# Layer 1's key chain: four split float32r products a head, or weights multiplied first in plain float32

## The chip, the cores and the metric

The kernel runs on one core of a Trainium2 chip. The metric is the device time of one execution in microseconds (us): before the change the median of 3 runs is 1177.97 us (1175.52 to 1180.46). The profiled execution took 1178.59 us and its recorded span is 1176.8 us, so 1.79 us lie around the span.

## The reference, cut to what matters

Four layers follow each other, each with an attention over a short context and a feed-forward stage; the stages run one after the other. The change lies in the attention of layer 1. Its mathematics, for 16 heads h, on the context `kv_rope` (4 batches of 64 rows, 64 wide, with the rotary tables applied):

```python
q_hk   = (hidden_q @ Wq.T).reshape(b, s, H, K)            # Wq: (16*128, 256)
q_big  = einsum('bshk,hkq->bshq', q_hk, w_kc_q)           # w_kc_q[h]: 128 x 192
q_r    = einsum('bshq,hqr->bhsr', q_big, W_qr)            # W_qr[h]: 192 x 64
k_r    = einsum('bld,hdr->bhlr', kv_rope, W_kr)           # W_kr[h]: 64 x 64
scores = einsum('bhsr,bhlr->bhsl', q_r, k_r)
attn   = softmax(scores)
ctx_c  = einsum('bhsl,bld->bhsd', attn, kv_rope)
out    = einsum('bhsd,hkd->bshk', ctx_c, w_kc_kv).reshape(b, s, H*K) @ Wo.T
```

Layer 1 puts no rotation on the queries, so everything that does not depend on them can be folded to the side of the keys: G[h] = Wq[h].T · w_kc_q[h] · W_qr[h] · k_r[h].T, a 256 x 256 block a head (256 model columns; 4 batches of 64 context rows), and Y[h] = w_kc_kv[h].T · Wo[:, h].T. The scores are then the normed x times G.

## The kernel before, in words

`latent_chain` (line 1056) computes G and Y before layer 1's attention. It takes the 16 heads in 4 rounds of two pairs, four heads a round. Every operand exists as two float32r tiles, a high part and the remainder, and `mm3` (line 79) forms a product as high·high + high·low + low·high, three matmuls.

Per round TensorE runs 14 steps: two steps of keys `KR` (W_kr by the context, 128 rows to 64), two of `Y`, four of `UU` (W_qr by KR, 64 rows to 96 twice), two of `VV` (w_kc_q by UU, 96 rows) and four of G (Wq by VV, 128 rows). That is 32 products of 256 columns, 96 matmuls. They go to the four PSUM banks of `PB` in turn. After each step ScalarE copies the bank to the high part (line 1122 or 1124) and VectorE subtracts it from the bank for the low part (line 1144 or 1147). The next step in the chain waits for that low part (`free`, line 1157).

The weights of a round come in four sections on SyncE's queue (line 1100) into one buffer `W`, whose memory is the tile STAGE and is shown as ffn_STAGE. ScalarE copies each section to `WS_hi` (`high`, line 1111) and GpSimd subtracts for `WS_lo` (line 1107); TensorE waits for `w_lo`. The next round's section may be loaded when GpSimd has split the last one. ScalarE does this splitting between its evictions, at the steps named in `AFTER`. GpSimd, ScalarE, VectorE and TensorE run their rounds in hardware loops, TensorE with its first round written out.

The layer's norm (`norm`, line 203) is done ahead of the rounds: ScalarE takes the standard deviation (line 235), VectorE normalizes 8 tiles (line 223), TensorE transposes them in 16 matmuls into the banks `NB` (line 247), ScalarE and VectorE split them (lines 240 and 229). Nothing in the rounds needs the result; `attend` (line 1202), which follows behind a barrier of all engines, does: its first score matmul reads G and the transposed x.

Of the kernel before, what the change touches and what calls it, by code (L numbers as in the profile page):

```python
# [15 lines left out]
P = 128  # L16
F32 = mybir.dt.float32
# [3 lines left out]
ALU = mybir.AluOpType  # L21
# [8 lines left out]
H = 16  # L30
# [13 lines left out]
CQ_N = {0: 2 * CQ, 1: 2 * 2 * K}  # L44


def pair_columns(layer):
    o_kr = O_CQ + CQ_N[layer]
# [37 lines left out]
def program(nc, A, out, rows_dram):  # L86
    with ExitStack() as top:
# [165 lines left out]
        def latent_rope(Y, AT):  # L253


            o_qr, o_kr, o_ck, o_wo, width = pair_columns(0)
# [799 lines left out]
        def latent_chain(GS, Y, W):  # L1056


            o_qr, o_kr, o_ck, o_wo, width = pair_columns(1)
            with ExitStack() as ctx:  # L1060
                WS = split(ctx, "WS", [P, 2, width])
                KR = split(ctx, "KR", [P, 4, B * L])
                UU = split(ctx, "UU", [ROT, 4, 2, B * L])
                VV = KR
                PB = psum(ctx, "PB", [P, 4, 512])
                NB = psum(ctx, "NB", [P, 4, 512])
                nrm = norm(ctx, "a1", [NB[:, j, :] for j in range(4)])

                SECTIONS = (slice(o_kr, o_qr), slice(o_qr, width), slice(O_CQ, o_kr), slice(O_WQ, O_CQ))
                NS = len(SECTIONS)  # L1070
                w_in = [sem(ctx, f"w_in_{c}") for c in range(NS)]
                w_hi, w_lo = sem(ctx, "w_hi"), sem(ctx, "w_lo")
                in_ps, part_hi, part_lo = sem(ctx, "in_psum"), sem(ctx, "part_hi"), sem(ctx, "part_lo")
                STEPS = 2 + 2 + 4 + 2 + 4
                ROUNDS = NP // 2

                def place(s, g):

                    if s < 2:
                        return R, 512, [part[0:R, 2 * s:2 * s + 2, :].rearrange("p h n -> p (h n)") for part in KR]  # L1080
                    if s < 4:
                        return P, D, [part[:, bass.ds(g * (2 * D) + (s - 2) * D, D)] for part in Y]
                    if s < 8:
                        return ROT, 512, [part[:, s - 4, :, :].rearrange("p q n -> p (q n)") for part in UU]
                    if s < 10:
                        return P, 512, [part[:, 2 * (s - 8):2 * (s - 8) + 2, :].rearrange("p h n -> p (h n)") for part in VV]
                    return P, 512, None

# [1280 lines left out]
```

## Time and profile before

| | |
|---|---|
| median of 3 runs | 1177.97 us |
| lowest, highest | 1175.52, 1180.46 us |
| profiled execution, its own time | 1178.59 us |
| its span | 1176.8 us |
| granted TensorE clock, mean over the span | 0.918 |
| PE busy | 1000.2 us |
| stage of the chain, from the last matmul of the stage ahead to the first score matmul | 577.4 to 649.74 us |

Engines are PE (TensorE's matmuls), PEld (its weight loads), DVE (VectorE), ACT (ScalarE), POOL (GpSimd) and SP (SyncE, DMA queue). A granted clock of 0.5 is TensorE at 1.2 GHz and 1.0 at 2.4 GHz. The ends of matmuls are modelled and overlap, so the step from one start to the next tells what one costs. A plain float32 matmul leaves two records (two weight loads and two passes), a float32r one leaves one; float32r tiles are often shown as f32. A "window" row gives busy time of each engine and its count of instructions in a stretch.

### The profile page before, as it was taken

To read this page: it belongs to the slowest core of one execution; us is meant where nothing else is said; L and a number is where in the kernel's file an instruction comes from. 1 tells how busy PE (TensorE), PEld (TensorE's weight loads), DVE (VectorE), ACT (ScalarE), POOL (GpSimd) and SP (SyncE) were. 2 spreads that over 40 slices of the span, in tenths; PEclk is the share of its full clock that TensorE was granted. 3 is DMA by queue.
4 is the path that set the end of the run, shared out by engine and by line. 5 is a ranking of instruction groups with operands and counts; after the bars stand their busy time and mean duration, and the time that the engine had idled before them with its cause. 6 is when DMAs were issued, how large, how long until landed. Compare 5 with 4: busy or idle time off the path is not lost. (4 is left out here: it accounts for less than half of the span.)

```text
span 1176.8 us, 14937 instructions
## 1 busy us (share of the span) xinstructions
PE 1000.2 (85%) x5309; PEld 809.6 (69%) x5309; DVE 690.7 (59%) x1133; ACT 387.6 (33%) x589; POOL 394.5 (34%) x258
## 2 busy tenths in 40 slices
PE   2999999867879999999688895967826769999997
PEld 2778787667669988888688794755715656566664
DVE  5466666455475655555556797967677864222221
ACT  2234342232413333333277432433313332211221
POOL 2576766300212222222075120153226320512222
PEclk9899999979889999999789997869966997999999
DMA  4111110001101111110242101000010009622220
GB/s 125 58 38 39 50 64 0 1 1 53 45 27 45 45 45 45 45 45 18 80 162 80 72 1 32 1 1 1 1 41 1 1 24 402 263 63 39 40 36 10
DMA packets 22817, 62.85 MB, mean 53 GB/s; under 512 B 4465, under 2 KB 13954, under 8 KB 20418
## 3 DMA queue, kind: packets, MB, share of 16 engines
q1 hardware_dynamic: 18690, 58.00, 14.1%
q0 software_dynamic: 4080, 4.22, 2.1%
q8 instruction: 30, 0.49, 0.2%
q14 instruction: 17, 0.14, 0.0%
HBM read 56.94 MB, written 9.21 MB: 56 GB/s over the span
## 5 line engine op out<-in xcount | busy, mean ns | idle before, releaser
L791 ACT ACTIVATE ffn_HG<-ffn_G,ffn_UB 128x512 f32<-128x512 f32 x54 | 37.1, 690 | 160.5 <-PE ffn_U L83 160.1
L761 POOL TENSOR_TENSOR ffn_WDS_lo<-ffn_WD,ffn_WDS_hi 128x1024 fp32r<-128x1024 f32 x9 | 22.1, 2457 | 200.3 <-ACT ffn_WDS_hi L781 200.3
L908 DVE SCALAR_TENSOR_TENSOR ffn_HF<-ffn_U,ffn_BIAS,ffn_HG 128x512 f32<-128x512 f32 x54 | 40.4, 751 | 82.6 <-ACT ffn_HG L791 82.4
L81 PE MATMUL ffn_DN<-ffn_WDS_hi,ffn_HS_hi 128*128 128x256 f32 x288 | 83.7, 290 | 3.9 <-DVE ffn_HS_lo L916 3.3
L2158 PE MATMUL ffn_GU<-ffn_W,ffn_XTB 128*128 x184 | 85.0, 605 | 0.3 <-issue 0.3
L82 PE MATMUL ffn_DN<-ffn_WDS_lo,ffn_HS_hi 128*128 128x256 f32 x288 | 83.3, 289 | 0.0
L83 PE MATMUL ffn_DN<-ffn_WDS_hi,ffn_HS_lo 128*128 128x256 f32 x288 | 83.2, 289 | 0.0
L923 DVE SCALAR_TENSOR_TENSOR X<-ffn_DN,ffn_CG,X 128x256 f32<-128x256 f32 x144 | 67.3, 481 | 20.6 <-PE ffn_DN L83 12.5
L1978 POOL DMA_INDIRECT out_x<-ffn_YB,ffn_XB x23 | 35.9, 1560 | 113.8 <-DVE ffn_YB L2107 111.8
L458 DVE TENSOR_TENSOR attn_RP<-attn_QB,attn_COS 96x1024 f32<-96x1024 f32 x32 | 39.0, 1217 | 51.3 <-PE attn_QB L83 51.2
L2096 DVE COPY ffn_XTB<-ffn_XP 128x256 f32<-128x256 f32 x23 | 9.8, 425 | 88.1 <-PE ffn_XP L2167 88.1
L81 PEld LDWEIGHTS ffn_DN<-ffn_WDS_hi,ffn_HS_hi 128*128 128x128 f32 x288 | 57.1, 198 | 5.2 <-DVE ffn_HS_lo L916 3.5
L564 PE MATMUL attn_ST<-attn_RP,attn_U 96*128 96x256 f32 x256 | 60.3, 385 | 0.0
L2185 PE MATMUL ffn_DN<-ffn_W,ffn_HT 128*128 (+1 forms) x248 | 58.7, 380 | 0.8 <-ACT ffn_HT L2003 0.8
L2158 PEld LDWEIGHTS ffn_GU<-ffn_W,ffn_XTB 128*128 128x128 f32 x184 | 33.1, 189 | 36.2 <-issue 33.7
L82 PEld LDWEIGHTS ffn_DN<-ffn_WDS_lo,ffn_HS_hi 128*128 128x128 f32 x288 | 57.2, 199 | 0.6
L83 PEld LDWEIGHTS ffn_DN<-ffn_WDS_hi,ffn_HS_lo 128*128 128x128 f32 x288 | 57.1, 198 | 0.0
L81 PE MATMUL attn_QB<-XT_hi,attn_C_hi 128*96 128x512 f32 x128 | 55.9, 437 | 1.2 <-DVE attn_C_lo L449 1.2
L1107 POOL TENSOR_TENSOR chain_WS_lo<-ffn_STAGE,chain_WS_hi 128x1024 fp32r<-128x1024 f32 (+2 forms) x16 | 42.4, 2665 | 37.6 <-ACT chain_WS_hi L1113 37.4
L350 POOL TENSOR_TENSOR attn_RP<-attn_RP,attn_RS 96x512 f32<-96x512 f32 x32 | 41.0, 1282 | 34.8 <-DVE attn_RS L462 34.8
L564 PEld LDWEIGHTS attn_ST<-attn_RP,attn_U 96*128 96x128 f32 x256 | 48.1, 193 | 6.6
L83 PE MATMUL attn_QB<-XT_hi,attn_C_lo 128*96 128x512 f32 x128 | 51.9, 406 | 0.0
(439 smaller groups left out, 2966.6 us busy)
## 6 DMA issues: line engine op xcount, KB each, us to landing
ffn_W<-in_f_w SPq DMA_DIRECT2D x9, 1536.0 KB, 27.6
attn_W<-in_L_pairs SPq DMA_DIRECT2D x8, 1088.0 KB, 5.0
ffn_WU<-in_f_up SPq DMA_DIRECT2D x9, 768.0 KB, 4.2
ffn_WD<-in_f_down SPq DMA_DIRECT2D x9, 512.0 KB, 3.5
ffn_STAGE<-in_L_pairs SPq DMA_DIRECT2D x8, 512.0 KB, 3.9
ffn_STAGE<-in_L_pairs SPq DMA_DIRECT2D x4, 896.0 KB, 4.7
expert_rows<-in_rows_empty SPq DMA_DIRECT2D x1, 2967.0 KB, 14.4
ffn_XB<-expert_rows SPq DMA_DIRECT2D x23, 129.0 KB, 2.1
```

Source lines behind the costliest of these rows:

```text
L81: pe.matmul(out, a[0], b[0], start=first, stop=False)
L82: pe.matmul(out, a[0], b[1], start=False, stop=False)
L83: return pe.matmul(out, a[1], b[0], start=False, stop=last)
L350: pool.tensor_tensor(RP[:, u, 0, :], RP[:, u, 0, :], RS[:, u % 2, 1, :], ALU.add).then_inc(rope_add, 1)
L458: dve.tensor_tensor(RP[:, u, :, :].rearrange("p q (b s) -> p q b s", b=2), src, cos, ALU.mult).then_inc(rope_mul, 1)
L564: last = pe.matmul(ST[:, half, b * S:(b + 1) * S], U[:, h, q, 2 * half + b, :], RP[:, u, q, b * S:(b + 1) * S], start=u < 2 and b == 0 and ...
L791: act.activation(HG[:, k % 2, :], G[:, k % 2, :], ACT.Silu, bias=bias).then_inc(silu_done, 1)
L908: dve.scalar_tensor_tensor(out=HF[:, k % 2, :], in0=U[:, k % 2, :], scalar=BIAS[:, bass.ds(e * (2 * NC) + 2 * m + 1, 1)], in1=HG[:, k % 2, ...
L923: ins = dve.scalar_tensor_tensor(out=X[:, t, :], in0=DN[:, q, o * D:(o + 1) * D], scalar=CG[:, :, :].rearrange("p e t -> p (e t)")[:, bass ...
L1107: pool.tensor_tensor(WS[1][:, :, cols], W[:, :, cols], WS[0][:, :, cols].bitcast(F32), ALU.subtract).then_inc(w_lo, 1)
L2158: last = pe.matmul(GU[:, m, :], x, weights(e, k * 2 * HID3 + m * HID3, HID3), start=k == 0, stop=k == KD - 1)
L2185: last = pe.matmul(DN[:, n % 2, 0:D], HT[:, n % 2, c * P:(c + 1) * P], weights(e, UPW + c * D, D), start=c == 0, stop=c == HID3 // P - 1)
```

## The change

Layer 1's chain is reordered and its products are in plain float32 on unsplit weights. For each head it now forms A = w_kc_q · W_qr (128 x 64; two matmuls of 64 columns over 96 rows), BT = A.T · Wq (64 x 256; both heads of a pair in one 128-wide tile, in which AF has zeros beside each head's 64 columns), KR (both heads of a pair at once, over 64 rows), and G = BT.T · KR (two matmuls of 256 columns over 64 rows, from partitions 0 to 63 or 64 to 127). Y is formed as before. Only Y and G, which the attention reads, are still split in two parts. A second weight buffer WB is added; the weights arrive in three sections, with no split on ScalarE and GpSimd. The norm is moved: deviation first on ScalarE, the normalizing on VectorE inside round 0, the transposes on TensorE behind round 1, in the banks of G. All loops are written out. Host code lays out the weights in the new order (`fold_pairs`); layer 0 is as it was.

```diff
-                WS = split(ctx, "WS", [P, 2, width])
-                KR = split(ctx, "KR", [P, 4, B * L])
-                UU = split(ctx, "UU", [ROT, 4, 2, B * L])
+                WB = sbuf(ctx, "WB", [P, 2, F_END])
+                AF = sbuf(ctx, "AF", [P, 2, 2, 192])
+                KVF = sbuf(ctx, "KVF", [DC, B * L])
+                BT = sbuf(ctx, "BT", [P, 2, D])
+                KR = sbuf(ctx, "KR", [P, 2, B * L])
                 PB = psum(ctx, "PB", [P, 4, 512])
-                NB = psum(ctx, "NB", [P, 4, 512])
+                GB = psum(ctx, "GB", [P, 4, 512])
+                SECTIONS = ((0, ROT, slice(F_QR, F_WQ)), (1, P, slice(F_WQ, F_CK)), (2, P, slice(F_CK, F_END)))
+                NORM_AFTER = 1
                     def _(sp):
                         for g in range(ROUNDS):
-                            for c, cols in enumerate(SECTIONS):
-                                if g > 0:
-                                    sp.wait_ge(w_lo, NS * (g - 1) + c + 1)
+                            for c, rows, cols in SECTIONS:
+                                if g >= 2:
+                                    sp.wait_ge((kr_ps, bt_ps, y_ps)[c], g - 1)
+                                sp.dma_start(W2[g % 2][0:rows, :, cols], A["L1_pairs"][2 * g:2 * g + 2, 0:rows, cols].rearrange("a p n -> p a n")).then_inc(w_in[c][g % 2], 16)
                     def _(pool):
-                        with pool.Fori(0, ROUNDS) as g:
-                            for c, cols in enumerate(SECTIONS):
-                                pool.wait_ge(w_hi, NS * g + c + 1)
-                                pool.tensor_tensor(WS[1][:, :, cols], W[:, :, cols], WS[0][:, :, cols].bitcast(F32), ALU.subtract).then_inc(w_lo, 1)
+                        pool.memset(AF[:, :, :, :].rearrange("p a j n -> p (a j n)"), 0.0).then_inc(padded, 1)
+                        pool.tensor_tensor(KVF[:, :], KV[0][0:DC, :].bitcast(F32), KV[1][0:DC, :].bitcast(F32), ALU.add).then_inc(kv_whole, 1)
                     def _(act):
                         nrm["deviation"](act)
+                        for g in range(ROUNDS):
+                            act.wait_ge(kr_ps, g + 1)
+                            if g > 0:
+                                act.wait_ge(g_ps, 4 * g)
+                            act.activation(KR[:, :, :].rearrange("p a n -> p (a n)"), PB[:, 1, :], ACT.Copy).then_inc(kr_sb, 1)
+                            act.wait_ge(y_ps, g + 1)
+                            act.activation(y_part(g, 0), PB[:, 3, :], ACT.Copy).then_inc(y_hi, 1)
+                            for h in range(4):
+                                act.wait_ge(g_ps, 4 * g + h + 1)
+                                act.activation(g_part(g, h, 0), g_bank(h), ACT.Copy).then_inc(g_hi, 1)
+                            if g == NORM_AFTER:
+                                nrm["scalar"](act)
                     def _(dve):
+                        dve.wait_ge(padded, 1)
+                        for g in range(ROUNDS):
+                            dve.wait_ge(a_ps, g + 1)
+                            if g > 0:
+                                dve.wait_ge(bt_ps, g)
+                            dve.tensor_copy(AF[:, :, :, 0:R], PB[:, 0, 0:4 * R].rearrange("p (a j r) -> p a j r", a=2, j=2)).then_inc(a_sb, 1)
+                            dve.wait_ge(bt_ps, g + 1)
+                            if g > 0:
+                                dve.wait_ge(g_ps, 4 * g)
+                            dve.tensor_copy(BT[:, :, :].rearrange("p a n -> p (a n)"), PB[:, 2, :]).then_inc(bt_sb, 1)
+                            if g == 0:
+                                nrm["vector"](dve)
+                            dve.wait_ge(y_hi, g + 1)
+                            dve.tensor_tensor(y_part(g, 1), PB[:, 3, :], y_part(g, 0).bitcast(F32), ALU.subtract).then_inc(y_lo, 1)
+                            for h in range(4):
+                                dve.wait_ge(g_hi, 4 * g + h + 1)
+                                dve.tensor_tensor(g_part(g, h, 1), g_bank(h), g_part(g, h, 0).bitcast(F32), ALU.subtract).then_inc(g_lo, 1)
+                            if g == NORM_AFTER:
+                                nrm["vector_low"](dve)
                     def _(pe):
+                            for a in range(2):
+                                for j in range(2):
+                                    for q in range(2):
+                                        last = pe.matmul(PB[:, 0, (2 * a + j) * R:(2 * a + j + 1) * R], w(a, F_CQ + (2 * j + q) * K, K, ROT), w(a, F_QR + (2 * j + q) * R, R, ROT), start=q == 0, stop=q == 1)
+                            last.then_inc(a_ps, 1)
+                            for a in range(2):
+                                last = pe.matmul(PB[:, 1, a * 256:(a + 1) * 256], w(a, F_KR, 2 * R, DC), KVF[:, :], start=True, stop=True)
+                            last.then_inc(kr_ps, 1)
+                            pe.wait_ge(w_in[1][g % 2], loads)
+                            pe.wait_ge(a_sb, g + 1)
+                            for a in range(2):
+                                for j in range(2):
+                                    last = pe.matmul(PB[:, 2, a * D:(a + 1) * D], AF[:, a, :, :].rearrange("p j n -> p (j n)")[:, P * j:P * (j + 1)], w(a, F_WQ + D * j, D), start=j == 0, stop=j == 1)
+                            last.then_inc(bt_ps, 1)
+                            for a in range(2):
                                 for j in range(2):
+                                    last = pe.matmul(PB[:, 3, a * D:(a + 1) * D], w(a, F_CK + P * j, P), w(a, F_WO + D * j, D), start=j == 0, stop=j == 1)
+                            last.then_inc(y_ps, 1)
+                            pe.wait_ge(bt_sb, g + 1)
+                            pe.wait_ge(kr_sb, g + 1)
+                            if g == NORM_AFTER + 1:
+                                pe.wait_ge(nrm["ready"], 4)
+                            for a in range(2):
+                                for j in range(2):
+                                    h = 2 * a + j
+                                    if g > 0:
+                                        pe.wait_ge(g_lo, 4 * (g - 1) + h + 1)
+                                    for k in range(KD):
+                                        last = pe.matmul(GB[:, h, k * 256:(k + 1) * 256], BT[R * j:R * (j + 1), a, k * P:(k + 1) * P], KR[R * j:R * (j + 1), a, :], start=True, stop=True)
+                                    last.then_inc(g_ps, 1)
+                        for g in range(ROUNDS):
+                            step(g)
+                            if g == NORM_AFTER:
+                                pe.wait_ge(g_lo, 4 * g + 4)
+                                nrm["tensor"](pe)
```

## Rows read from the trace of the kernel before

**Rows 1.** The page's engine line: busy time, share of the span, instructions.
```profile
PE 1000.2 (85%) x5309; PEld 809.6 (69%) x5309; DVE 690.7 (59%) x1133; ACT 387.6 (33%) x589; POOL 394.5 (34%) x258
```

**Rows 2.** Windows: from:to, length, busy PE, PEld, DVE, ACT, POOL (count), clock, DMA share, GB/s.
```profile
590.06:606.72 16.66, 14.63 (x97) 13.75 (x97) 10.14 (x18) 11.70 (x20) 13.65 (x6) 0.85 0.57 185
606.72:621.21 14.49, 12.49 (x97) 11.60 (x97) 8.74 (x15) 11.37 (x19) 10.63 (x5) 1.00 0.52 165
635.70:647.90 12.20, 12.20 (x96) 11.55 (x96) 8.13 (x13) 7.85 (x14) 3.42 (x2) 1.00 0.00 1
```

**Rows 3.** Timeline, 577 to 590 us: start, length, engine, line, operation, [idle before, releaser].
```profile
579.53 10.88 SPq L1100 DMA_DIRECT2D ffn_STAGE<-in_L_pairs  x5
...
582.82 3.68 PE L247 MATMUL chain_NB<-IDENT,XN 128*128 128x128 f32 x16 [5.46 <-DVE XN L223]
582.89 1.39 DVE L223 TENSOR_SCALAR XN<-X,MOM,RSTD 128x256 f32<-128x256 f32 x4
584.26 3.44 ACT L1113 ACTIVATE chain_WS_hi<-ffn_STAGE 128x1792 fp32r<-128x1792 f32 x3 [2.94 <-DMA ffn_STAGE<-in_L_pairs]
586.04 5.77 POOL L1107 TENSOR_TENSOR chain_WS_lo<-ffn_STAGE,chain_WS_hi 128x1792 fp32r<-128x1792 f32 x2 [26.91 <-ACT chain_WS_hi L1113]
587.94 1.06 ACT L1113 ACTIVATE chain_WS_hi<-ffn_STAGE 128x1024 fp32r<-128x1024 f32 x1 [0.23 <-DMA ffn_STAGE<-in_L_pairs]
...
590.06 0.48 PE L81 MATMUL chain_PB<-KV_hi,chain_WS_hi 128*64 128x256 f32 x1 [3.56 <-POOL chain_WS_lo L1107]
```

**Rows 4.** The page's DMA issues: count, KB of each, us to landing.
```profile
ffn_STAGE<-in_L_pairs SPq DMA_DIRECT2D x4, 896.0 KB, 4.7
```

**Rows 5.** Timeline at the end of a round, and of the last one.
```profile
634.95 1.29 DVE L1147 TENSOR_TENSOR chain_GS_lo<-chain_PB,chain_GS_hi 128x512 f32 x2 [0.63 <-ACT chain_GS_hi L1124]
635.70 0.33 PE L81 MATMUL chain_PB<-KV_hi,chain_WS_hi 128*64 128x256 f32 x1 [1.57 <-DVE chain_GS_lo L1147]
...
646.56 2.85 DVE L1147 TENSOR_TENSOR chain_GS_lo<-chain_PB,chain_GS_hi 128x512 f32 x4 [0.38 <-ACT chain_GS_hi L1124]
647.66 0.28 PE L83 MATMUL chain_PB<-chain_KR_hi,chain_WS_lo 128*128 128x256 f32 x1
649.74 0.47 PE L81 MATMUL attn_SC<-chain_GS_hi,XT_hi 128*128 128x512 f32 x1 [1.81 <-PEq L1093]
```

**Rows 6.** Timeline: float32 matmuls of other stages, by their own count of records.
```profile
65.43 1.89 PE L564 MATMUL attn_ST<-attn_RP,attn_U 96*128 96x256 f32 x8
...
840.11 1.04 PE L1464 MATMUL attn_TR<-IDENT,attn_E 128*128 128x128 f32 x8
...
972.44 5.91 PE L2134 MATMUL ffn_LG<-ffn_RW,XN 128*128 128x8 f32 x27
```

**Rows 7.** The page's groups: busy us, mean ns of one, idle before.
```profile
L564 PE MATMUL attn_ST<-attn_RP,attn_U 96*128 96x256 f32 x256 | 60.3, 385 | 0.0
...
L2096 DVE COPY ffn_XTB<-ffn_XP 128x256 f32<-128x256 f32 x23 | 9.8, 425 | 88.1 <-PE ffn_XP L2167 88.1
```

**Rows 8.** Timeline of PE where full-height matmuls give way to 64-row ones.
```profile
609.50 0.28 PE L83 MATMUL chain_PB<-chain_WS_hi,chain_WS_lo 128*128 128x256 f32 x1
609.71 0.35 PE L81 MATMUL chain_PB<-chain_KR_hi,chain_WS_hi 64*96 64x256 f32 x1
609.90 0.28 PE L82 MATMUL chain_PB<-chain_KR_lo,chain_WS_hi 64*96 64x256 f32 x1
610.02 0.28 PE L83 MATMUL chain_PB<-chain_KR_hi,chain_WS_lo 64*96 64x256 f32 x1
```

**Rows 9.** Windows, columns as in Rows 2: where the granted clock is low.
```profile
590.06:594.90 4.84, 4.84 (x23) 4.84 (x24) 3.36 (x7) 2.45 (x5) 4.84 (x3) 0.50 0.73 255
...
972.50:979.20 6.70, 6.70 (x34) 6.70 (x33) 0.69 (x1) 1.15 (x1) 0.00 (x0) 0.50 1.26 494
...
841.00:843.80 2.80, 0.17 (x3) 0.03 (x1) 2.60 (x8) 1.02 (x1) 1.90 (x1) 1.00 0.00 0
843.80:847.50 3.70, 3.70 (x14) 3.23 (x15) 0.00 (x0) 1.02 (x1) 0.00 (x0) 0.55 0.00 0
```

More of the change, by code:

```diff
@@ L43, with pair_columns @@
 O_CQ = O_WQ + 2 * D
-CQ_N = {0: 2 * CQ, 1: 2 * 2 * K}
-def pair_columns(layer):
-    o_kr = O_CQ + CQ_N[layer]
+F_QR = 0
+F_CQ = F_QR + 2 * 2 * R
+F_KR = F_CQ + 2 * 2 * K
+F_WQ = F_KR + 2 * R
+F_CK = F_WQ + 2 * D
+F_WO = F_CK + 2 * P
+F_END = F_WO + 2 * D
+def pair_columns():
+    o_kr = O_CQ + 2 * CQ
     o_ck = o_kr + 2 * R
@@ new lines, in latent_chain @@
+                WB = sbuf(ctx, "WB", [P, 2, F_END])
[3 more added lines that the diff above has]
+                KR = sbuf(ctx, "KR", [P, 2, B * L])
+                PB = psum(ctx, "PB", [P, 4, 512])
+                GB = psum(ctx, "GB", [P, 4, 512])
+                nrm = norm(ctx, "a1", [GB[:, j, :] for j in range(4)])
+                W2 = (W, WB)
+                ROUNDS = NP // 2
@@ L1127, in _ @@
-                        nrm["deviation"](act)
-                        for c in range(NS):
-                            high(0, c)
-                        nrm["scalar"](act)
-                        with act.Fori(0, ROUNDS - 1) as g:
-                            step(g)
-                        step(ROUNDS - 1, last=True)
+                        nrm["deviation"](act)
+                        for g in range(ROUNDS):
[10 more added lines that the diff above has]
+                                nrm["scalar"](act)
@@ L2285, in pairs @@
         w[p, :, O_WQ + D * j:O_WQ + D * (j + 1)] = Wq[h * K:(h + 1) * K]
-        if layer == 0:
-            w[p, :, O_CQ + CQ * j:O_CQ + CQ * (j + 1)] = w_kc_q[h]
-        else:
-            for q in range(2):
-                c = O_CQ + 2 * K * j + K * q
-                w[p, :ROT, c:c + K] = w_kc_q[h][:, ROT * q:ROT * (q + 1)].T
+        w[p, :, O_CQ + CQ * j:O_CQ + CQ * (j + 1)] = w_kc_q[h]
         w[p, :R, o_qr + CQ * j:o_qr + CQ * (j + 1)] = W_qr[h].T
@@ L2295, in pairs, with fold_pairs @@
         w[p, :, o_wo + D * j:o_wo + D * (j + 1)] = Wo[:, h * K:(h + 1) * K].T
+    return w
+def fold_pairs(Wq, w_kc_q, w_kc_kv, W_qr, W_kr, Wo):
+    w = np.zeros((NP, P, F_END), np.float32)
+    for h in range(H):
+        p, j = divmod(h, 2)
+        for q in range(2):
+            c = 2 * j + q
+            w[p, :ROT, F_QR + R * c:F_QR + R * (c + 1)] = W_qr[h][ROT * q:ROT * (q + 1)]
+            w[p, :ROT, F_CQ + K * c:F_CQ + K * (c + 1)] = w_kc_q[h][:, ROT * q:ROT * (q + 1)].T
+        w[p, :DC, F_KR + R * j:F_KR + R * (j + 1)] = W_kr[h]
+        w[p, :, F_WQ + D * j:F_WQ + D * (j + 1)] = Wq[h * K:(h + 1) * K]
+        w[p, :, F_CK + P * j + DC * j:F_CK + P * j + DC * (j + 1)] = w_kc_kv[h]
+        w[p, :, F_WO + D * j:F_WO + D * (j + 1)] = Wo[:, h * K:(h + 1) * K].T
     return w
```

130 lines of the change are left out of this document (35 added, 95 removed).

## The prediction

> **What bounds the kernel now.** I read the page's engine line first: TensorE has a matmul in flight for 85% of the span [rows 1]. The stages follow each other behind barriers, so what the change is worth is read from its own stage alone: from the last matmul of the stage ahead (577.4 us) to the first score matmul (649.74 us). The windows of that stage come next [rows 2]: a middle round lasts 14.49 us with TensorE in flight for 12.49 of them (96 matmuls and one of the next round); a third such round follows at the same length, and the last one takes 12.2 us, all of it busy, for the same 96. So TensorE bounds the rounds, and some 2.2 us a round are waits that vanish where ScalarE has no weights to split in between: in the last round its busy time is 7.85 instead of 11.37 us. Then the timeline of the front [rows 3]: the first load is issued at 579.53 and used at 584.26, but the first product starts at 590.06, since ScalarE's copies and GpSimd's subtractions come between. Last, the ends of rounds [rows 5]: TensorE stands still for 1.57 us for the low part of G, and after the last matmul's start (647.66) it takes 2.08 us to the first score matmul.
>
> Before the change, then: products start at 590.06, the last one streams until 647.66 + 0.12 = 647.8, scores start at 649.74.
>
> **The front.** The split on ScalarE and GpSimd goes, so the first product waits for its load alone. The first section was 896 KB [rows 4] and was in use at 584.26; the other 1408 KB of the round were there at 587.94, when ScalarE's last copy stopped waiting for them: 380 KB a us [rows 3]. The new first section is 2 x 96 x 896 x 4 bytes = 672 KB, 0.6 us less: 583.7, and 583.8 for the first matmul, against 590.06: **6.3 us gained**. The other sections (512 and 768 KB) follow by 585.1 and 587.1, each ahead of its use, below. Round 1's three loads queue behind them, and from round 2 on SyncE's queue waits for KR, BT and Y of two rounds earlier, with only later loads behind the wait; 1.95 MB are wanted a round, some 10 us, where the trace shows 255 GB/s [rows 9]. I cost that at nothing. GpSimd's two new instructions (768 columns of zeros, 256 of a sum over 64 rows) are cheaper than 1024 of the 2560 columns that it subtracts in 5.77 us [rows 3]: under 2.3 us, beside 4.2 us of loading.
>
> **One float32 product of 256 columns.** Layer 0 has the same kind over 96 rows [rows 6]: 8 records in 1.89 us. The last one's own length is 0.38 [rows 7], so a step is (1.89 - 0.38)/7 = 0.216 us and a product, two records, 0.43 us, at the full clock. An old product of three matmuls is 3 x 0.12 = 0.36 [rows 8]. A round has 2 (KR) + 4 (BT) + 4 (Y) + 8 (G) = 18 such products: **7.8 us**, for 32 x 0.36 = 11.5 before.
>
> **The eight small ones for A.** 64 columns over 128-wide weights; such a form is not in the trace. Nearest above is the row with 8 columns, where the weight load must set the pace: 27 records in 5.91 us, less 0.36 for the last, over 26 = 0.213 us, at half clock [rows 6, 9]. Transposes of 128 columns, also with a 128-wide load each, run at full clock at no more than 1.04/8 = 0.13 [rows 6]. I take 0.11 a record, half of 0.213; 16 records are **1.75 us** a round. Below is 0.054 (64 columns at the 256-column rate), above 0.213: 3.6 us less or 6.6 us more over the four rounds.
>
> **Changes of height.** KR and G are over 64 rows, A, BT and Y are not: four changes a round, 15 in all. At one such change the next matmul starts 0.21 us after its forerunner and the one behind it 0.19 later, for a step of 0.12 [rows 8]: 0.16 us lost; the way back is alike. I take 0.19 each, as two-record products may lose a little more: **2.9 us** (0 to 0.4 each: 0 to 6).
>
> **Waits inside a round.** BT waits for AF, which VectorE copies only behind G's low parts of the round before. In the last round VectorE ends 646.56 + 2.85 = 649.41, so 1.63 us after TensorE's last column (647.78) [rows 5]. A takes 1.75 + 0.19 and its result is seen some 0.2 later; the copy of 256 columns is 0.43 [rows 7]: done 2.6 us after G. TensorE, with A, KR (0.87) and two changes, is there at 3.2: hidden, with 0.6 us to spare. BT's copy (0.65 to 0.7, as the subtractions of 512 columns [rows 5]) hides behind Y's 1.73. In round 0 VectorE has the normalizing in between, twice 1.39 and two reciprocals, 3.1 us [rows 3]: its copy for round 1 comes 8.0 us after BT of round 0, TensorE at 8.6. Nothing, but a margin of half a us; without it the excess is paid once. ScalarE has 3.6 us of copies a round.
>
> **The norm.** Its 16 transposes took place under the loading and now stand behind round 1: TensorE waits for G's last low part, 1.63 + 0.11 = 1.75 us (it is 1.57 today, at every round [rows 5]), then 16 x 0.11 = 1.75. **3.5 us added.** The rest of the norm runs beside A and KR of round 2, in the place of G's low parts in the reckoning above.
>
> **The clock.** Today products start at half clock, for 4.84 us [rows 9]. TensorE again comes from several us without work, so I keep a cold start, and as A comes first and the weight-load-bound row above stayed at 0.50 for all its 6.7 us though TensorE was never idle [rows 9], I take 6 us of it: 3.0 us lost (4.8 us: 2.4; A's cold 3.4 us and 4.8 more: 4.1).
>
> **The sum.** Four rounds of 7.8 + 1.75 = 38.2; changes 2.9; norm 3.5; clock 3.0: 47.6 us for what took 57.7. Gained 10.1, with the front **16.4 us**. The stretch from the last column to the scores stays, since the same copy and subtraction end it. 1178.59 - 16.4 = 1162.2 for the profiled execution, whose own time lies 0.6 above the median: **1161.6 us**.
>
> **A second fall of the clock.** After a pause of 2.6 us the clock fell to half as work resumed, for most of the next 3.7 us; after pauses of 1.57 at the ends of rounds it did not [rows 9, 5, 2]. At the norm there are 1.75 us of pause, then transposes, then A's thin columns. If it falls, 3.4 us at half clock cost 1.7: **1163.3**. The Trainium skill ("TensorE: Matmul & The Clock Gate", Part 4) says that transposes do not count as busy for the clock gate as matmuls do; the 16 transposes at 582.82, all at half clock in 3.68 us, agree, and no row shows them at a fall. Chance 0.25.
>
> **Two heights at once.** G's products alternate between partitions 0 to 63 and 64 to 127, two and two. If the array can start one half while the other streams, each of the three borders in a round saves one record's 0.216: 0.65 a round, 2.6 in all: **1159.0**. Nothing in the trace shows two such products side by side. The Trainium skill ("TensorEngine Tiling (Array Packing)", Key Properties) says that tiles of different row groups can load and multiply in parallel, and also that a change of tiling mode drains the array; the second is what the 0.16 us at a change agree with. Chance 0.12.
>
> **A's records do not speed up with the clock.** At 0.213 also when warm, about 14 more records a round pay 0.1 in three and a half rounds: 5.7 us, **1167.3**. For it: the only row where the load sets the pace is a cold one; against it: the warm transposes. Chance 0.08.
>
> **The chain gains nothing.** If waits between the four engines, now each at a product twice as long, fill what the fewer products save, only the front is left: 1177.97 - 6.3 = **1171.7**. Against it: 0.6 us to spare at the tightest wait. Chance 0.06.
>
> **Slower.** The clock never rises in this stage, as it did not in the 6.7 us with 8 columns [rows 9]. Then 38.2 + 2.9 + 1.75 of work take twice as long, 42.9 more, for the 3.0 already counted: 39.9 - 16.4 = 23.5 slower, **1201.5**. It turns the sign once some 39 us of the stage are at half clock (19.4 us of gain without any, 0.5 a us). Against it: A is 1.75 of some 10 us a round, and layer 0's float32 products run at full clock [rows 6]. Chance 0.03.
>
> **How the numbers follow.** The forecast has 0.46. The range of 8 in 10 takes in the first three rivals and the bounds of A and of the changes in part: 1155 to 1168. Faster by over 0.5% (5.9 us, about what a measurement of this kernel can tell; beyond 1172.1): forecast, the first three rivals and most of the fourth, 0.94; within it 0.03; slower 0.03.
>
> **What would show it.** The first product near 583.8 us on the same scale, with a wait for the DMA alone. Records of 256 columns 0.216 apart, A's 0.11. A round from A to A of some 10.3 us. One pause of 1.75 us ahead of the transposes, none above 0.3 elsewhere. Scores at some 633.4. Granted clock below 1.0 once, up to about 589.8. Wrong it would be by A's step, by a second stretch at 0.5, or by a wait of BT for AF at each round.

## The result, and the profile after

The changed kernel takes 1166.12 us in the median of 4 runs (1163.92 to 1167.16), the kernel before on the same chip 1177.88; the ratio is 0.9897, 95% interval 0.9876 to 0.9919. Its profiled execution took 1165.65 us, with a span of 1163.9 us and a mean granted clock of 0.911 (0.918 before). The forecast was 1161.6 us: of the 16.4 us expected, 11.8 came in the medians and 12.9 in the spans.

First the profile's engine line of the changed kernel, as in [rows 1]:

```profile
PE 990.9 (85%) x5133; PEld 795.6 (68%) x5133; DVE 672.4 (58%) x1105; ACT 354.6 (30%) x541; POOL 353.8 (30%) x244
```

PE is busy 9.3 us less in the whole span. In the stage itself, from the last matmul of the stage ahead to the first score matmul, it is busy 11.0 us less (55.52 before, 44.56 now) and idle 4.2 us less: 1.2 of these 4.2 ahead of the first product, 3.0 behind it, where waits for the other engines went. The timeline of the front of the stage, for [rows 3]:

```profile
580.31 1.36 SPq L1102 DMA_DIRECT2D ffn_STAGE<-in_L_pairs  x3
580.32 0.74 POOL L1106 MEMSET chain_AF<- 128x768 f32 x1 [20.41 <-POOLq L740]
581.02 0.72 POOL L1107 TENSOR_TENSOR chain_KVF<-KV_hi,KV_lo 64x256 f32<-64x256 f32 x1
581.72 2.15 SPq L1102 DMA_DIRECT2D chain_WB<-in_L_pairs  x3
585.98 3.67 PE L1160 MATMUL chain_PB<-ffn_STAGE 96*128 96x64 f32 x16 [7.83 <-DMA ffn_STAGE<-in_L_pairs]
```

The first product waits for its load alone and starts 5.67 us behind the issue of it; before it was 10.53. Then PE through the four rounds, one row for each group of products (A is L1160, KR L1167, BT L1175, Y L1182, G L1194, the norm's transposes L253):

```profile
589.58 2.07 PE L1167 MATMUL chain_PB<-chain_KVF,ffn_STAGE 64*128 64x256 f32 x4
591.59 3.78 PE L1175 MATMUL chain_PB<-ffn_STAGE,chain_AF 128*128 128x256 f32 x8
595.16 2.20 PE L1182 MATMUL chain_PB<-ffn_STAGE 128*128 128x256 f32 x8
597.29 2.10 PE L1194 MATMUL chain_GB<-chain_KR,chain_BT 64*128 64x256 f32 x16
599.32 2.00 PE L1160 MATMUL chain_PB<-chain_WB 96*128 96x64 f32 x16
...
602.52 3.65 PE L1175 MATMUL chain_PB<-chain_WB,chain_AF 128*128 128x256 f32 x8
...
607.83 2.10 PE L1194 MATMUL chain_GB<-chain_KR,chain_BT 64*128 64x256 f32 x16
612.16 3.07 PE L253 MATMUL chain_GB<-IDENT,XN 128*128 128x128 f32 x16 [2.23 <-DVE chain_GS_lo L1143]
615.03 2.48 PE L1160 MATMUL chain_PB<-ffn_STAGE 96*128 96x64 f32 x16
...
622.15 2.10 PE L1194 MATMUL chain_GB<-chain_KR,chain_BT 64*128 64x256 f32 x16
624.18 2.00 PE L1160 MATMUL chain_PB<-chain_WB 96*128 96x64 f32 x16
626.11 1.13 PE L1167 MATMUL chain_PB<-chain_KVF,chain_WB 64*128 64x256 f32 x4
627.17 1.99 PE L1175 MATMUL chain_PB<-chain_WB,chain_AF 128*128 128x256 f32 x8
629.00 1.89 PE L1182 MATMUL chain_PB<-chain_WB 128*128 128x256 f32 x8
630.82 2.10 PE L1194 MATMUL chain_GB<-chain_KR,chain_BT 64*128 64x256 f32 x16
635.42 0.48 PE L87 MATMUL attn_SC<-chain_GS_hi,XT_hi 128*128 128x512 f32 x1 [2.50 <-PEq L1095]
```

Read the starts. In the last round A takes 1.93 us (624.18 to 626.11), KR 1.06, BT 1.83 and Y 1.82. But G's 16 records end 2.10 us behind their start, in every round, where Y's 8 records of the same 256 columns take 1.89: half of G costs next to nothing. Two waits stand in brackets, 2.23 us ahead of the transposes and 2.50 ahead of the scores. And the same work is longer at some places than at others: BT 3.65 in round 1 and 1.99 in round 3. The windows tell why. Their columns are those of [rows 2]; the granted clock stands third from the end:

```profile
582.10:595.70 13.60, 9.72 (x30) 7.96 (x31) 0.72 (x2) 0.60 (x2) 0.00 (x0) 0.50 1.03 313
602.50:606.00 3.50, 3.48 (x9) 2.78 (x10) 0.00 (x0) 0.51 (x1) 0.00 (x0) 0.51 0.75 176
612.90:616.30 3.40, 3.40 (x19) 3.40 (x18) 2.47 (x4) 2.35 (x4) 0.00 (x0) 0.51 0.01 4
636.70:640.10 3.40, 3.40 (x11) 2.75 (x10) 0.29 (x1) 0.00 (x0) 0.00 (x0) 0.50 0.74 299
...
616.30:632.90 16.60, 16.60 (x99) 13.44 (x98) 6.59 (x12) 5.37 (x10) 0.00 (x0) 1.00 0.00 1
```

The clock is at half (1.2 GHz) for the first 9.8 us of the products (585.98 to 595.77), and falls again three times, twice in this stage and once in the scores behind it. The kernel before had none of these three falls.

**The account.** From the issue of the first load to the first score matmul the stage took 70.21 us (579.53 to 649.74) and takes 55.11 (580.31 to 635.42): 15.1 less. The stage begins 0.78 us later, and what follows the first score takes 1.4 more (528.5 for 527.1 us; the fall in the scores, 3.4 us at half clock, is worth 1.7): 12.9 us stay in the span.

### The profile page after: what moved, and what is told of

Its sections match the earlier page's. It is cut to its first block and busy times, and to the rows that moved or that the text cites. A ratio compares the mean times of both kernels' runs of the same rounds, so it can differ in the third digit from the quotient of the medians.

```text
span 1163.9 us, 14272 instructions
## 1 busy us (share of the span) xinstructions
PE 990.9 (85%) x5133; PEld 795.6 (68%) x5133; DVE 672.4 (58%) x1105; ACT 354.6 (30%) x541; POOL 353.8 (30%) x244
## 5 line engine op out<-in xcount | busy, mean ns | idle before, releaser
L88 PE MATMUL attn_QB<-XT_lo,attn_C_hi 128*96 128x512 f32 x128 | 51.9, 405 | 0.0
```

What stands on the lines that cost most here:

```text
L88: pe.matmul(out, a[0], b[1], start=False, stop=False)
```

## The experiments

All times of a stage below run from the issue of its first load to the first score matmul, as above (55.11 us in the changed kernel). Where the record of that first matmul is missing, its start is put 0.3 us ahead of the second's, as in the changed kernel. A stage's time is that of one profiled execution, which can lie off its kernel's median (by 3.8 us in the kernel without A, 3.2 in the one with A over 128 columns). The code shown is cut to the operands that change.

### Both heads of a pair from one half of the array

The theory: G's products alternate between partitions 0 to 63 and 64 to 127, and the two halves run side by side. Here all read the lower half: the same work, but every second head gets the G of its neighbour.

```diff
-BT[R * j:R * (j + 1), a, k * P:(k + 1) * P], KR[R * j:R * (j + 1), a, :]
+BT[0:R, a, k * P:(k + 1) * P], KR[0:R, a, :]
```

> Every product of G reads partitions 0 to 63 of BT and KR, also those of the odd heads (their G is wrong; the work is the same). Theory one, two heights at once: in the changed kernel G's 16 records of a round take 2.10 us because heads of the two halves of the array run side by side; here they go one behind the other, 15 x 0.216 + 0.38 = 3.6 us a round, 6.1 us more over four rounds. ScalarE and VectorE then keep up with TensorE, so the pause ahead of the transposes goes from 2.2 back to 1.75 us and the one ahead of the scores from 2.5 back to 1.8: 1.2 us less. If the falls of the clock at 602.6, 612.8 and 636.6 us came because TensorE is less busy with G side by side, one to three of them go, 1.7 us each: a median between 1166 and 1171 us against 1166.1 of the changed kernel. Theory two, a product over 64 rows is fast by itself: G still takes 2.1 us and the time stays at 1166.

Measured: 1167.78 us, ratio 0.9927 (0.9907 to 0.9946); the stage took 58.07 us. Its PE timeline, the last round and the transposes:

```profile
608.67 3.58 PE L253 MATMUL chain_GB<-IDENT,XN 128*128 128x128 f32 x16 [1.41 <-DVE chain_GS_lo L1143]
...
622.32 2.00 PE L1160 MATMUL chain_PB<-chain_WB 96*128 96x64 f32 x16
...
628.96 3.72 PE L1194 MATMUL chain_GB<-chain_KR,chain_BT 64*128 64x256 f32 x16
```

The same 16 records take 3.72 us for 2.10: side by side is shown, at 1.62 us a round. A round from A to A is 10.28 us here (612.04 to 622.32), and 10.3 were forecast without side by side. Yet of these 6.5 us in four rounds only 3.0 show in the stage's time. Two waits are shorter: that for the last low part of G is 1.41 us here and 2.23 in the changed kernel, likewise the one at the end (1.68 and 2.50), since VectorE's low parts follow each other no faster than every 0.60 us a head when G comes at double pace. Together that is 1.6. There is also one fall of the clock in this stage (608.8 to 612.2), not two, which is 1.7, and no wait for AF in round 1, 0.2: 6.5 - 3.5 = 3.0.

### The same order, grouped by halves

Heads 0 and 2 first (lower half), then 1 and 3 (upper half), with the evictions in that order.

```diff
-for a in range(2):
-    for j in range(2):
-        h = 2 * a + j
+for i, h in enumerate((0, 2, 1, 3)):
+    for a, j in (divmod(h, 2),):
```

> G's heads in the order 0, 2, 1, 3, so both heads of the lower half first and both of the upper half behind them. As the prediction reckoned it (a product can start beside its forerunner, but not ahead of it), only one border is left: G takes 14 x 0.216 + 0.38 = 3.4 us a round. If TensorE looks as far ahead as eight records, it still takes 2.1 us. If it looks ahead less far, between the two.

Measured, a single run: 1161.76 us. G takes 2.96 us a round: with one border between the halves instead of three, 0.76 us of 1.62 are left. That is some 3.5 records of 0.216: the second half starts about four records ahead of its turn, which is one head's worth. Alternating head by head comes close to the full gain (8 steps of 0.216 and the end of the last record would be 1.9 us, an estimate from these rows; 2.10 were measured), and grouping does not. The clock fell twice here too: in round 1 (598.4 to 601.8) and in the scores, but not at the transposes, which followed a pause of 1.64 us.

### Without A

A's products and the copy of them are left out; BT is computed from the zeros in AF.

```diff
-for a, j, q: last = pe.matmul(PB[:, 0, ...], w(a, F_CQ ...), w(a, F_QR ...))
-last.then_inc(a_ps, 1)
-dve.tensor_copy(AF[:, :, :, 0:R], PB[:, 0, 0:4 * R]...).then_inc(a_sb, 1)
```

> The products of A and their copy are left out (AF stays zero, so G is zero). In the changed kernel the clock rises 9.7 us after the first product. Theory one, A's 64-column products hold it down, as the weight-load-bound row of before did: here KR and BT come first and the clock rises 3.4 to 5.9 us after the first product, and the falls at 602.6 and 612.8 go: A's own time of 3.7 + 2.0 + 2.5 + 2.0 = 10.2 us, plus 2 to 3 us for the shorter cold start, plus 1.7 to 3.4 for the falls, so 14 to 16.5 us under the changed kernel, 1150 to 1152. Theory two, the clock has nothing to do with A: only the 10 us go, 1156, and the clock rises more than 8 us after the first product.

Measured: 1151.75 us, ratio 0.9794 (0.9773 to 0.9814), stage 41.84 us, 13.3 less. Windows of it:

```profile
581.00:588.30 7.30, 6.31 (x14) 4.67 (x15) 0.42 (x1) 0.60 (x1) 0.00 (x0) 0.50 1.04 310
588.30:619.10 30.80, 26.07 (x151) 20.92 (x151) 20.28 (x38) 14.29 (x27) 0.00 (x0) 1.00 0.53 160
```

A's own steps in the changed kernel are 3.60 us at half clock and 1.93 at full, 9.4 in four rounds. Of the other 3.9, 3.4 are the two falls of the stage, which are gone. The rest, 0.5, is about the wait for AF in round 1 (0.2) and the changes of height between A and its neighbours. The clock rises 6.4 us behind the first product instead of 9.8, but those 3.4 us are A's half-clock products, already counted: behind the start of KR it rises 6.4 us here and 6.2 there. This rise lies between what the two theories named. The transposes follow the same pause of 2.23 us and run at full clock, 1.97 us for 16. So the small products for A cost 9.4 us, of which 1.7 is the half clock of the first ones, and the falls are no price of that pause alone.

### Products ahead of the first load

Twelve products of 512 columns on data that is there already fill part of the wait for the load; nobody reads them.

```diff
+for i in range(12):
+    pe.matmul(PB[:, 0, :], KVB[0][:, i % B, :], XT[0][:, 0, 0:512], start=True, stop=True)
 for g in range(ROUNDS):
     step(g)
```

> Twelve idle products of 512 float32r columns into the bank of A, on data that are there, ahead of round 0 (5.1 us at half clock, in place of the 5.6 us wait for the first load). Theory one: dense columns raise the clock, so that it is at full speed when the first load lands or within 2 us of it, against 9.7 us before: 3.5 to 4.8 us gained, 1161.3 to 1162.6 us. If the later falls stay where they are relative to the work. Theory two, the clock does not rise from work that is not followed by more, or A's thin columns let it fall again at once: 1165 to 1167 us, and the granted clock is 0.5 in A of round 0.

Measured: 1162.11 us, ratio 0.9872 (0.9852 to 0.9893), stage 55.13 us: nothing in the stage.

```profile
578.90:582.10 3.20, 3.04 (x12) 2.18 (x12) 0.00 (x0) 1.77 (x3) 1.42 (x2) 1.00 0.63 153
584.10:594.30 10.20, 9.73 (x30) 7.97 (x31) 0.72 (x2) 0.60 (x1) 0.00 (x0) 0.50 1.05 330
```

The filling ran at full clock, then came 2.59 us of waiting for the load; the clock fell 0.5 us ahead of A and rose 9.7 us behind A's start, practically as without the filling (9.8). The falls stood where they stand in the changed kernel, 22.2, 32.5 and 56.4 us behind the first issue.

### A over 128 columns

Each of A's products streams both heads' 64 columns (the second 64 are not read), so that a record streams as many columns as its weights have.

```diff
-PB[:, 0, (2 * a + j) * R:...], w(a, F_CQ ...), w(a, F_QR + (2 * j + q) * R, R, ROT)
+PB[:, 0, (2 * a + j) * 2 * R:...], w(a, F_CQ ...), w(a, F_QR + (2 * j + q) * R, 2 * R, ROT)
```

> Each product of A streams 128 columns in place of 64 (its own 64 and the 64 behind them, whose result is not used); weight loads, count and order of the products are as in the changed kernel. Where the weight load sets the pace, at 0.11 us a record at full clock and 0.21 at half, 128 columns fit into the same time, so A's rows should stay at 2.0 us (warm) and 3.7 (cold). Theory one, it is the share of time in which columns stream that the clock follows: the clock rises 5 to 6.5 us after the first product in place of 9.7, and the fall in round 1 (602.6 us in the changed kernel) goes: 1.6 to 2.3 + 1.7 us gained, 1162 to 1163. The falls behind the two pauses may stay. Theory two, the weight loads or the pauses matter: nothing moves, 1166. Theory three, a record of 128 columns is slower than 0.11: 32 records a microsecond each way, A takes 16 x 0.13 and more, 1167 or above.

Measured: 1160.78 us, ratio 0.985 (0.982 to 0.988), stage 53.09 us, 2.0 less. Its row for the first A, and the window in which the clock is at half:

```profile
585.88 3.78 PE L1160 MATMUL chain_PB<-ffn_STAGE 96*128 96x128 f32 x16 [8.07 <-DMA ffn_STAGE<-in_L_pairs]
```

```profile
580.42:594.07 13.65, 8.19 (x26) 6.69 (x27) 0.42 (x1) 2.13 (x4) 1.17 (x2) 0.50 0.97 288
```

Twice the columns cost 0.1 us at half clock (3.78 for 3.67) and 0.05 at full (2.05 for 2.00): it is not the columns that set the pace of A but, at both levels of the clock, most likely the weight load, which is the same 128 wide. The clock rose 8.2 us behind the first product instead of 9.8 (0.8 us gained), and the fall of round 1 did not come (1.7); BT of round 1 waited 0.2 us longer for AF, and the wider records cost some 0.3 in all.

That the width did this isn't shown by this run. The clock was at half for 13.65 us here as in the changed kernel (582.12 to 595.77), but from 0.25 us behind the first issue on, where in the changed kernel's profile, and in its second one, it was 1.8 us. The earlier rise is that earlier beginning, and the missing fall may be too. A cleaner pair comes below, with the norm ahead.

### The norm ahead of the rounds

ScalarE and VectorE do the normalizing and TensorE the transposes while the first load is on its way, as in the kernel before.

```diff
+nrm["tensor"](pe)
 for g in range(ROUNDS):
     step(g)
-    if g == NORM_AFTER:
-        pe.wait_ge(g_lo, 4 * g + 4)
-        nrm["tensor"](pe)
```

> The norm is done ahead of the rounds again, as in the kernel before: the transposes stand in the 5.6 us wait for the first load. They end about 7.7 us after the first load is issued (3.3 to the first, 3.7 at half clock, some 0.3 over), so the first product comes 1.4 to 2.0 us later than in the changed kernel (5.67 us after the issue). The pause of 2.23 us and the transposes behind round 1 (3.07 us) go, and so does the fall at 612.8 us, 1.7 us of which the transposes' own half-clock time is part. Net from the first issue to the scores: 55.1 - 5.2 - 0.9 + 1.7 = 50.7 us, a median near 1162. Rival: VectorE's longer work ahead of A's copy in round 0 delays BT, or the clock's rise comes later by the same 1.5 us, and the gain is 2 us or less, 1164 and above.

Measured: 1157.3 us, ratio 0.9821 (0.9788 to 0.9854), stage 48.07 us, 7.0 less. The timeline:

```profile
577.77 1.36 SPq L1102 DMA_DIRECT2D ffn_STAGE<-in_L_pairs  x3
...
579.63 1.38 DVE L229 TENSOR_SCALAR XN<-X,MOM,RSTD 128x256 f32<-128x256 f32 x4
...
581.07 3.67 PE L253 MATMUL chain_GB<-IDENT,XN 128*128 128x128 f32 x16 [5.42 <-DVE XN L229]
...
584.53 3.52 PE L1157 MATMUL chain_PB<-ffn_STAGE 96*128 96x64 f32 x16
```

The transposes end 1.1 us behind the load, so A starts at 6.76 us for 5.67. What goes for that 1.1 us: the wait and the transposes behind round 1 (5.2 us from G's end to A, with a fall in them), the rest of that fall in A of round 2 (0.5), the fall and the wait for AF in round 1 (1.9), and 0.6 in round 0, where the clock rises sooner behind A's start: 8.1 in all, less 1.1 is 7.0. From its rise at 593.3 the clock stays up through the first scores. All rounds behind the first take 8.67 us.

### The first load over 128 partitions

```diff
-SECTIONS = ((0, ROT, slice(F_QR, F_WQ)), ...
+SECTIONS = ((0, P, slice(F_QR, F_WQ)), ...
```

> The first section is loaded over all 128 partitions (896 KB instead of 672, the lower 32 rows hold zeros). The first product came 5.67 us after the first issue in the changed kernel, where the prediction had 4.3. If the 96 partitions load the 16 engines unevenly, the first product now comes 4.7 to 5.0 us after the issue, as the same size did before the change (4.7). If not, 6.0 to 6.4 us, for the larger size.

Measured, a single run: the first product starts 5.21 us behind the issue, 0.46 earlier though a third more is moved (896 KB for 672). Neither theory gave that number. The stage took 51.35 us, 1161.25 in all; no fall came in it, and the transposes behind the same 2.23 us of pause ran at full clock.

### Round 1's loads held back

SyncE issues the loads of round 1 only when the first section has landed.

```diff
 for c, rows, cols in SECTIONS:
+    if g == 1 and c == 0:
+        sp.wait_ge(w_in[0][0], 16)
```

> Round 1's loads are issued only once the first section has landed. If the six loads queued at once slow the first one down, the first product comes 4.3 to 4.8 us after the first issue; if not, at 5.6 to 5.7 as before. Round 1's data, wanted 13 us later, are there in either case.

Measured, a single run: 1164.71 us, the first product 5.71 us behind the issue. Round 1's loads, queued behind, don't slow the first. Windows from 1.5 to 4.5 us behind the first issue, in this kernel and then in the one with the load over 128 partitions:

```profile
577.22:580.22 3.00, 0.00 (x0) 0.00 (x0) 0.00 (x0) 0.30 (x2) 0.00 (x0) 0.59 0.94 251
580.46:583.46 3.00, 0.00 (x0) 0.00 (x0) 0.00 (x0) 0.30 (x2) 0.00 (x0) 0.55 0.90 328
```

The 16 DMA engines are as busy (0.94 and 0.90 on average) but move 251 GB/s for 328; the changed kernel moves 241 in its own such window and the kernel before, whose first section is over 128 partitions too, 348. So the load over 96 partitions is slower by its rate, and not because engines stand idle. Why the rate is lower isn't shown.

The stage took 58.41 us, since the fall at the transposes lasted three times as long:

```profile
598.30:601.70 3.40, 3.40 (x10) 2.66 (x9) 0.19 (x1) 0.26 (x1) 0.00 (x0) 0.50 0.79 195
608.50:618.70 10.20, 10.20 (x37) 8.71 (x36) 3.10 (x5) 2.73 (x5) 0.00 (x0) 0.50 0.00 1
```

### The changed kernel again

Three kernels with the same work on TensorE (the changed one, and the last two) had two, no and two falls in the stage, of different length. Is it chance?

> The changed kernel itself once more, for a second look at the clock's falls. The same instructions in the same order fell at the norm's pause, in round 1 and in the first scores before (3.4 us at half clock each). Theory one, the falls are set by the program: the same three falls within 0.5 us, stage from the first load issue to the first score matmul 55.1 us. Theory two, they hang on where the chip's clock stands in its own rhythm when the stage begins, which differs from run to run: falls at other places or in another number, stage anywhere from 51.4 to 58.5 us, as three kernels with the same TensorE work have shown. I expect theory two, and a median of some 1166 in either case.

Measured: 1163.18 us, ratio 0.9878 (0.9855 to 0.99). My expectation fell: the clock fell 22.3, 32.5 and 56.4 us behind the first issue, to within 0.2 us as the first time, for 3.4 us each, and the stage took 55.1 us. So in two profiled executions of one program the falls came at the same places. In kernels whose timing is shifted a little (0.46 us earlier in the one, an issue held back in the other) they lay elsewhere or were missing. The executions without a profile needn't be alike: of the eight of this kernel four have the mean granted clock of the profiled ones, 0.911, and four have 0.914 or 0.917.

### The halves again, where nothing falls

The norm ahead of the rounds and all of G from the lower half (as above, every second head gets its neighbour's).

> The norm ahead of the rounds, and all products for G read the lower 64 partitions (the odd heads' G is then that of the wrong half: the output is not the reference's). It prices the two halves of the array side by side where no fall of the clock blurs it. Theory one, the 1.62 us a round that G takes less with alternating halves are real time: G 3.72 us a round instead of 2.10, stage 48.07 + 6.5 - 0.8 (shorter pause before the scores) = 53.8 us, time some 1157.3 + 5.7 = 1163. Theory two, the evictions hide most of it, since ScalarE and VectorE lag behind G anyway and the next round waits for them: stage 50 to 51 us, time some 1160.

Measured: 1162.65 us, ratio 0.987 (0.9847 to 0.9893), stage 53.7 us (579.00 to 632.69) against 48.07: 5.6 us for side by side, as theory one had it (6.5 less 0.8 of shorter wait). The evictions hide none of it between rounds, which take 10.29 us here and 8.67 there. The clock stayed up from its rise to the last product in both; in the scores behind, it was at half for 6.8 us here and never there.

### The norm ahead, and A over 128 columns

Both edits from above together, and a third kernel with the load over 128 partitions as well.

> The norm ahead of the rounds and A's products over 128 streamed columns. Theory one, wider streams let the clock rise earlier after the cold start, as with the norm in its old place (8.1 instead of 9.7 us behind the first product): 1.6 us less at half clock is 0.8 us less, stage 47.3 us, time 1156.5. Theory two, with the transposes ahead of A the rise is set by them, and nothing is left to gain: stage 48.1, time 1157.3.

> As the kernel with the norm ahead and the wide A, and the first section of each round is loaded over all 128 partitions instead of 96 (its last 32 hold zeros for A's weights and are not read). Theory one, the load over 128 partitions lands some 0.5 us earlier, as in the one look before (5.21 for 5.67 us from issue to first product), and the whole stage follows, since with the norm done nothing else holds A: stage 46.8 us, time 0.5 below its sibling. Theory two, A waits for the transposes and not for the load once these stand in the wait: no difference. A third way: 0.22 MB more to load a round delays the second section and costs 0.3 us.

Measured: 1153.06 us, ratio 0.9796 (0.9771 to 0.982), and 1153.28, ratio 0.9803 (0.9775 to 0.9831); the changed kernel on the same chip took 1163.18. Both stages took 45.0 us. The timeline of the first of the two, a window of it, and the window of the kernel with the norm ahead alone in which the clock is at half:

```profile
581.60 3.67 PE L253 MATMUL chain_GB<-IDENT,XN 128*128 128x128 f32 x16 [5.46 <-DVE XN L229]
585.07 2.83 PE L1157 MATMUL chain_PB<-ffn_STAGE 96*128 96x128 f32 x16
587.83 1.13 PE L1164 MATMUL chain_PB<-chain_KVF,ffn_STAGE 64*128 64x256 f32 x4
...
623.30 0.48 PE L87 MATMUL attn_SC<-chain_GS_hi,XT_hi 128*128 128x512 f32 x1 [2.50 <-PEq L1095]
```

```profile
581.60:586.90 5.30, 5.30 (x25) 5.30 (x26) 4.18 (x9) 2.39 (x4) 0.00 (x0) 0.50 1.04 325
579.62:593.28 13.66, 12.21 (x44) 10.64 (x45) 6.04 (x14) 2.99 (x5) 0.00 (x0) 0.50 1.03 307
```

The theory had 0.8 us for an earlier rise; it was 3.1, as the clock rose in the middle of A, 5.3 us behind the first transpose, where with 64 columns it took 12.2 (581.07 to 593.28). Here the beginning is the same: the clock had fallen 1.8 us behind the first issue in all four kernels with the norm ahead. It was at half for 6.83 us in the two with A at 128 columns and for 13.65 in the two with 64, so in this pair the width is what differs. The kernel with the load over 128 partitions gained nothing more: its A starts with the transposes' end, 6.75 us behind the issue, as theory two said. The first scores ran at half clock for 3.4 us in both. This is the fastest version, 0.9% below the changed kernel and 2% below the one before.

## Why the prediction was right, and where not

The direction and the range held; the forecast was 4.5 us too low. By its own signs the part on the clock was wrong: a second stretch at half came. Step by step:

| step | forecast | measured |
|---|---|---|
| first product behind the issue | 4.3 us | 5.67 |
| a product of 256 columns (Y: 4 in 1.73, and 0.1 for a change of height) | 0.43 | 0.43 |
| A, with a change of height | 1.94 a round | 1.93 |
| KR, with a change | 1.06 | 1.06 |
| a change of height | 0.19 | 0.19 |
| G, with its change | 3.65 | 3.64 from one half, 2.03 from two |
| a round without side by side | 10.3 | 10.28 |
| wait for AF | none | none but 0.2 in round 1 |
| pause at the norm | 1.75 | 2.23 |
| its transposes | 1.75 | 1.8 at full clock |
| half clock at the start | 6 us | 9.8 |
| falls after it | none | two in the stage, one in the scores |
| last column to first score | 1.96 | 2.66 |

The large terms, the rounds' work, were right to hundredths where G is read from one half. The price of A was among them, which no row of the kernel before showed: the value taken from the weight-load-bound row, halved for the full clock, was the right one. The rival that A's records don't speed up with the clock is out (0.11 us at full clock, 0.22 at half); its own sum was off besides, as 14 records at 0.1 us in three and a half rounds are 4.9 us and only 16 give about the 5.7 written. A change of height costs 0.09 us in the step ahead of it (Y's 1.82 us for 8 x 0.216 = 1.73) and 0.10 in the one behind (BT's 1.83): KR, between two changes, takes 1.06 us for 4 x 0.216 = 0.86. The rounds' gain came for the reason given: fewer products, 10.28 us of work with G from one half where the last round before took 12.20 and a middle one, with its waits, 14.49.

**Two heights at once** was named as a rival, with chance 0.12, and happened. The mechanism was right and its size was not: 0.65 us a round were priced, one record at each border, and it is 1.62, every second record. The step that failed is the one that let the array overtake only at a border: in the forecast itself side by side stood at nothing, and over four rounds it was 6.5 us. The Trainium skill ("TensorEngine Tiling (Array Packing)", Key Properties) says that different tiles can load and multiply in parallel; the 2.10 against 3.72 us agree with that. It names a drain at a change of mode too, and the 0.19 us at a change of height is all that the runs show of that.

**A second fall of the clock** was the other rival, with 0.25, and happened as well, at the named place and at another, and a third in the scores: 1.7 us each, as priced. The price of one was right, the number wrong, and so was the reason in part: the fall of round 1 has no such pause ahead of it, only the 0.2 us for AF. The two rivals have opposite signs and nearly cancel: 6.5 us for side by side, 5.1 for the falls. That the sum came near is in part luck.

**The cold start** was mis-sized by 3.8 us of half clock, 1.9 us of time, and lies above the forecast's own upper case (A's 3.4 us and 4.8 more). A took 3.6 us at half clock, as reckoned there; it is the part behind A that was 6.2 us and not 4.8. **The load** was mis-sized by 1.4 us: the rate of 380 KB a us was read from sections over 128 partitions and from the later of them. The forecast took 0.6 us off for fewer bytes; the runs show 0.46 more for the 96 partitions (5.67 for 5.21). The last 0.5 is that 896 KB over 128 partitions were in use 4.73 us behind the issue in the kernel before and 5.21 here (one run), and that stays open; 0.1 of the sum was allowed for in the forecast. **The pause** and the stretch to the scores were taken over from a G whose products come no faster than the evictions; with G from one half the pause is 1.41 us, with G at double pace 2.23, as the evictions keep theirs.

Added up against the 53.8 us forecast for the stage: load +1.4, cold start +1.9, two falls +3.4, side by side -6.5, norm's pause +0.5, AF +0.2, stretch to the scores +0.7: 55.4, for 55.11 measured. Outside of it what follows the first score (+1.4, with the fall there) and the 0.78 us at which the stage begins later make up the rest of the difference between 16.4 and 12.9. The last is scatter between executions: the second profile of the changed kernel issues its first load at 578.65, 0.88 us ahead of the kernel before.

Moving the norm behind round 1 was priced at 3.5 us and cost 7.0 in the profiled stage: at full clock 2.23 and 1.8, less the 1.1 us at which A starts earlier, are 2.9; two falls are 3.4, the later rise 0.5 and the wait for AF 0.2. The falls are no fixed price of that place: with the load over 128 partitions the norm stood there too and none came. Comparing the forecast's place for the norm with the place it left, under the load, would have been the better question.

## What to carry to other kernels

Products over at most 64 rows should alternate between the two halves of the partitions every few records, four here: the second half is nearly free (2.10 us for 3.72), as long as the evictions keep pace. Work that fits in the wait for a stage's first load should stay there, even where it ends a us behind the load; in the middle of a stage it brings a pause, and falls of the clock were seen there (5 of 7 profiles with the 2.23 us pause). Where small float32 products don't get faster with fewer columns, stream as many columns as the weights have: it cost 0.05 to 0.1 us a round here, and with the norm ahead the clock came up 6.9 us sooner.

## What the runs showed of the hardware

- 16 float32 records over 64 rows took 3.72 us from one half of the partitions, 2.10 alternating four by four, 2.96 in two blocks of eight. The array starts the other half some four records ahead.
- A change between 64-row and taller float32 products cost 0.19 us at full clock, 0.09 in the step ahead of it and 0.10 in the one behind.
- A record of float32 with 128-wide weights takes 0.11 us at full clock and 0.22 at half, whether it streams 64 or 128 columns.
- The clock rose 9.8 us behind the first product with A at 64 columns, 8.2 at 128 (where it had also fallen 1.6 us sooner); and 12.2 and 5.3 us behind the first transpose, with these ahead. The Trainium skill ("TensorE: Matmul & The Clock Gate", Part 4) says that transposes don't count as busy in the same way. If they did not count at all, the rise should lie as far behind A's start with them as without, 8.2 us at 128 columns; it was 1.9 in the kernel with both edits, and 1.8 in its sibling. At 64 columns it was 8.8 for 9.8, which is nearer to the rule.
- A fall behind the cold start lasted 3.4 us as a rule, once 6.8 and once 10.2. The same pause of 2.23 us ahead of the same transposes was followed by a fall in five profiles and by none in two (without A, and with the load over 128 partitions); a pause of 1.41 us was followed by one, a pause of 1.64 by none. In the two profiles of the changed kernel the places repeat. What decides between them stays open.
- A first load of 896 KB over 128 partitions was in use at 5.21 us, one of 672 KB over 96 at 5.67; in the window from 1.5 to 4.5 us behind the issue they moved 328 and 241 to 251 GB/s.
